# Attention with a routed expert gate on one Trainium2 core: values of two neighbouring pairs computed together from batch 1 on in place of batch 3

## The chip, the cores and the metric
The kernel is one program on one NeuronCore of a Trainium2 chip. The metric is device time in microseconds for one execution, lower is better. Engines: TensorE (PE, its weight loads PEld), VectorE (DVE), ScalarE (ACT), GpSimd (POOL), SyncE (SP, which issues most DMAs).

## What is computed
Eight batches of 256 tokens with 128 channels; 16 heads of size 64, latent key and value width 64; 8 experts.
```python
xn = layernorm(x)
q = rope(xn @ wq.T);  lat = xn @ w_kv_down.T
k = rope(lat @ w_k_up.T);  v = lat @ w_v_up.T
s = softmax(causal(q @ k.T / 8)) @ v @ wo.T          # per head, then joined
e = max(top2(xn @ gate_w + gate_b).indices)          # one expert per token
g = silu(2 * (gelu(xn @ w1[e] + b1[e]) @ w2[e] + b2[e]))
out = x + s * g
```

## The kernel before
**Slots.** The attention is cut into 64 slots g = 8 b + p: batch b of 8, pair of heads p of 8. Every engine has its own hand-written order of the slots (`slot(g)`), and semaphores tie the engines together. After slot 39 the experts run (22 tiles of 128 tokens), then slots 40 to 63, with the gate of each batch.

**One pair through the engines.** `project(m)` (TensorE) makes queries (m even) or keys (m odd) for two pairs, some 6 items ahead, so slot g projects m = g + 6. `rotate(m)` (VectorE, L585) multiplies the bank with the rotary table, and `rotated(m)` (GpSimd, L463) adds the halves; SyncE's `place` moves the result to `qk_sb`. `scores(g)` (TensorE, L1080 and L1082) is issued in slot g − 2. `row_max(g)` (VectorE, L594) adds the mask and takes row maxima, `exponentials(g, i)` (ScalarE, L885) follow for each head i of the pair, `denominators(g)` (VectorE, L601) is the reciprocal, `scale(g)` (GpSimd L474, in the slots with scatters and gathers partly VectorE L612 and ScalarE L898) makes the probabilities. `turn(g)` (TensorE, L1092) transposes them, `turned_probs(g)` (ScalarE, L907) copies them to `probsT`, which has four places. `values(g)` (TensorE, L1106 and L1108) multiplies them with the latents into `o_bank`, `ctx_out(g)` (ScalarE, L914) copies the result to `ctxT`, and `output(g)` (TensorE, L1120) multiplies by the joined value and output weights into `y_bank`. `take_y(b)` (VectorE, L761) copies a batch's eight summed outputs.

**Single and double values.** A pair in `ALONE` has its own call of `values`, with 256 and 128 columns a matmul, in slot g + 1, and its own copy in slot g + 2. Other pairs go by two, even and odd together: `values(g)` in slot g + 2 with 512 and 256 columns a matmul, one `ctx_out` of 512 columns in slot g + 3, then `output(g)` in slot g + 3 and `output(g + 1)` in slot g + 4. So with singles every slot has one call of `values`, and with doubles every even slot has one and the odd slots none. Before the change the pairs 0 to 23, 38, 39, 62 and 63 are alone.

**Order of work around it.** In `slot(g)` TensorE does scores(g + 2), project(g + 6), turn(g), some side work in early slots (input rows, latents, counts), output, values. VectorE does row_max(g + 2), denominators(g + 1), side work of the slot (statistics, normalisation, top 2, routing), and rotate(g + 6) last. In slots 8 to 20 all projections go into one bank, `j_bank`; from slot 20 on they alternate between two (`bank_of`). `project(m)` waits for `rope_done` at m while there is one bank (g up to TWO_J = 20), and at m − 1 from slot 21 on. In slots 22 to 37 GpSimd also issues a scatter of one tile of rows (L482).

Of the kernel before, what the change touches and what calls it, by code (L numbers as in the profile page):

```python
# [24 lines left out]
NP = H // 2  # L25
# [26 lines left out]
FINALS = {48: 0, 51: 5, 53: 1, 54: 2, 56: 3, 59: 6, 61: 4}  # L52
FINAL_ORDER = tuple(FINALS.values()) + (7,)
Z_PART = 18
FIRST_DOUBLE = 3 * NP
ALONE = tuple(range(FIRST_DOUBLE)) + (G_LEAD - 2, G_LEAD - 1, B * NP - 2, B * NP - 1)


# [37 lines left out]
def build(nc, x, wqT, w_dgT, w_kupT, w_vup, woT, gate_b, w1, b1, w2, b2,  # L96
          c_rot, c_ident, c_mask, c_before, c_expert, c_excl, c_incl, c_tile, out):
    with ExitStack() as ctx:
# [473 lines left out]
        def _(dve):  # L572
# [186 lines left out]
            def take_y(b):  # L759
                dve.wait_ge(y_step, NP * b + NP)  # L760
                dve.tensor_copy(y_keep[:, b, :], y_bank[:, 0:2 * C]).then_inc(y_read, 1)  # L761
# [16 lines left out]
            def slot(g):  # L778
                if 0 < g // NP < LEAD and g % NP == (2 if NP * (g // NP) <= FIRST_DOUBLE else 3):
                    take_y(g // NP - 1)  # L780
# [557 lines left out]
```

## Time and profile before

| | |
|---|---|
| Median of 3 runs (lowest, highest) | 310.27 us (310.02, 311.63) |
| Profiled execution: its time, its span | 311.37 us, 309.6 us |
| Busy, share of the span: PE, PEld | 96%, 77% |
| DVE, ACT, POOL | 71%, 78%, 70% |
| Mean granted TensorE clock | 0.985 of full speed |

The span goes from the first to the last instruction; the execution's own time holds what lies around it as well. Busy shares are averages over stages with different limits. Matmuls overlap in their pipeline, so the start of one group of matmuls to the start of the next says more about TensorE than the sum of durations.

### The profile page before, as it was taken

What the parts mean: (1) busy time and instruction counts of PE and PEld (TensorE: products, weight loads), DVE (VectorE), ACT (ScalarE), POOL (GpSimd) and SP (SyncE); (2) the same over time, 40 slices, a digit from 0 to 9 for tenths busy, and PEclk for the clock granted to TensorE, in tenths of its full rate; (3) what the DMA queues carried; (4) which work ended last, traced back from release to release, by engine and by line L of the source; (5) the groups of instructions that cost most, each with busy time, mean ns of one, the idle gap of its engine ahead of it and who ended that gap; (6) DMA issues with size and microseconds to landing.
All of it is one profiled execution on the core that took longest, in us unless ns stands there. A gap on an engine that the chain in (4) does not pass through costs nothing.

```text
span 309.6 us, 8479 instructions
## 1 busy us (share of the span) xinstructions
PE 296.1 (96%) x2358; PEld 237.5 (77%) x2358; DVE 221.1 (71%) x883; ACT 242.8 (78%) x851; POOL 215.8 (70%) x321
## 2 busy tenths in 40 slices
PE   8889999999999999999999989999989999899994
PEld 3578788888888888777777789999867777786763
DVE  4879998987787998988888523232268789898651
ACT  3376889898877789989897665555699999889982
POOL 3367978687777779999999943322138999889730
PEclk9987999999999999999999999999999999999998
DMA  6754595869433333333345470000063334344200
GB/s 207 231 135 112 96 263 151 216 168 298 113 69 71 65 73 86 95 87 87 88 101 138 124 210 0 2 2 0 3 186 71 89 103 112 105 109 131 74 18 18
DMA packets 39597, 33.35 MB, mean 108 GB/s; under 512 B 4802, under 2 KB 36675, under 8 KB 39555
## 3 DMA queue, kind: packets, MB, share of 16 engines
q1 hardware_dynamic: 38098, 30.51, 38.5%
q0 software_dynamic: 1024, 2.10, 2.5%
q8 instruction: 20, 0.33, 0.5%
q10 hardware_dynamic: 432, 0.23, 0.3%
q14 instruction: 23, 0.18, 0.2%
HBM read 11.07 MB, written 4.98 MB: 52 GB/s over the span
## 4 chain that ended last, share of the span: by engine, by line
PE 65%; POOL 12%; issue 11%; DVE 8%; ACT 2%; DMA 1%; POOLq 1%; SPq 0%; DVEq 0%; ACTq 0%
PE bank L1092 9%; PE bank L1080 9%; PE bank L1106 7%; PE bank L1120 6%; PE bank L1299 6%; PE bank L1284 6%; POOL probs L474 5%; POOL staged L463 4%; PE bank L1054 4%; PE bank L1082 3%; DVE rot_out L585 3%; PE bank L1108 3%; DVE masked L594 2%; PE bank L1070 2%; PE bank L1056 2%
## 5 line engine op out<-in xcount | busy, mean ns | idle before, releaser
L885 ACT ACTIVATE pexp<-masked,negmax 128x128 f32<-128x128 f32 (+1 forms) x256 | 114.1, 452 | 1.7 <-DVE negmax L594 1.6
L474 POOL TENSOR_SCALAR probs<-pexp,rden 128x256 f32<-128x256 f32 (+1 forms) x184 | 80.3, 451 | 27.0 <-DVE rden L601 24.2
L594 DVE CUSTOM_DVE_ANT_0 masked<-bank,mask 128x128 f32<-128x128 f32 (+1 forms) x256 | 75.9, 352 | 28.0 <-PE bank L1082 27.8
L463 POOL TENSOR_TENSOR staged<-rot_out 128x512 f32<-128x512 f32 x63 | 80.2, 1274 | 17.7 <-DVE rot_out L585 17.2
L585 DVE TENSOR_TENSOR rot_out<-bank,rot 128x1024 f32<-128x1024 f32 x64 | 77.7, 1215 | 4.0 <-PE bank L1056 2.7
L907 ACT COPY probsT<-bank 128x384 f32<-128x384 f32 x128 | 55.0, 480 | 23.8 <-PE bank L1092 23.2
L1092 PE MATMUL bank<-ident,probs 128*128 128x128 f32 x384 | 55.3, 278 | 1.8 <-ACT probsT L907 0.9
L885 ACT ACTIVATION_READ_ACCUMULATOR pexp<-masked,negmax 128x1 f32 x256 | 49.8, 195 | 0.0
L1080 PE MATMUL bank<-qk_sb 64*128 64x256 f32 x256 | 45.7, 434 | 2.6 <-DVE negmax L594 1.9
L1092 PEld LDWEIGHTS bank<-ident,probs 128*128 128x128 f32 x384 | 43.7, 141 | 5.0 <-POOL probs L474 1.8
L1120 PE MATMUL bank<-vo_sb,ctxT 128*128 128x128 f32 x256 | 39.5, 279 | 0.7 <-ACT ctxT L914 0.7
L1038 ACT ACTIVATE probsT<-bank,w_own 128x128 f32<-128x128 f32 x88 | 25.1, 368 | 18.8 <-PE bank L1284 18.8
L1106 PE MATMUL bank<-probsT,lat_all 128*64 128x256 f32 (+1 forms) x184 | 37.7, 488 | 0.3 <-ACT probsT L907 0.3
L1120 PEld LDWEIGHTS bank<-vo_sb,ctxT 128*128 128x128 f32 x256 | 33.7, 191 | 1.9 <-ACT ctxT L914 1.1
L549 POOL COPY w_own<-w_sb 128x516 f32 x22 | 13.5, 616 | 27.4 <-ACT probsT L1038 27.4
L1080 PEld LDWEIGHTS bank<-qk_sb 64*128 64x128 f32 x256 | 19.9, 188 | 16.2 <-issue 13.7
L1082 PEld LDWEIGHTS bank<-qk_sb 64*128 64x128 f32 x256 | 25.5, 190 | 2.7
L914 ACT COPY ctxT<-bank 128x256 f32<-128x256 f32 (+1 forms) x46 | 20.7, 451 | 6.8 <-PE bank L1108 5.6
L1082 PE MATMUL bank<-qk_sb 64*128 64x128 f32 x256 | 25.5, 275 | 0.0
L1299 PE MATMUL bank<-w_sb,probsT 128*128 x176 | 24.4, 282 | 0.7 <-issue 0.4
L1108 PEld LDWEIGHTS bank<-probsT,lat_all 128*64 128x64 f32 x184 | 13.3, 137 | 14.3 <-issue 10.3
L1284 PE MATMUL bank<-probsT,w_own 128*128 128x128 f32 x176 | 23.4, 277 | 0.7 <-DVE probsT L854 0.4
(113 smaller groups left out, 459.8 us busy)
## 6 DMA issues: line engine op xcount, KB each, us to landing
qk_sb<-staged SPq DMA_DIRECT2D x128, 128.0 KB, 2.6
w_sb<-in_w SPq DMA_DIRECT2D x2, 1024.0 KB, 5.8
w_sb<-in_w SPq DMA_DIRECT2D x4, 512.0 KB, 4.9
sorted_x<-z SPq DMA_DIRECT2D x1, 1408.0 KB, 7.9
sorted_g<-z SPq DMA_DIRECT2D x1, 1152.0 KB, 5.6
out<-res SPq DMA_DIRECT2D x8, 128.0 KB, 1.9
x_sb<-in_x SPq DMA_DIRECT2D x3, 256.0 KB, 3.2
rot<-in_c_rot SPq DMA_DIRECT2D x1, 512.0 KB, 5.6
```

What stands on the lines that cost most here:

```text
L463: pool.tensor_tensor(staged[:, n % 2, :, m % 2, :], rot_out[:, m % 2, :, 0:S], rot_out[:, m % 2, :, S:2 * S], op=ALU.add).then_inc(staged_ ...
L474: pool.tensor_scalar(probs[:, g % 2, i, c], pexp[:, g % 2, i, c], rden[:, g % 2, i, k:k + 1], 1.0, ALU.mult, ALU.mult).then_inc(probs_read ...
L585: dve.tensor_tensor(rot_out[:, m % 2], bank_of(m)[:].unsqueeze(1).broadcast_to([P, 2, 2 * S]), rot[:], op=ALU.mult).then_inc(rope_done, 1)
L594: t = dve.tensor_tensor_reduce(masked[:, g % 2, i, c], s_bank[i][:, c], mask[:, c], -1.0, -NEG * 1e8, ALU.add, ALU.min, negmax[:, g % 2, i ...
L885: e = act.activation(pexp[:, g % 2, i, c], masked[:, g % 2, i, c], ACT.Exp, bias=negmax[:, g % 2, i, k:k + 1], scale=-1.0, accum_out=rowsu ...
L907: act.copy(probsT[:, g % 4, i, :], t_bank[i][:, 0:SW]).then_inc(probsT_ready, 1)
L1080: pe.matmul(s_bank[i][:, P:SW], qk_sb[r, 0, p, P:S], qk_sb[r, 1, p, :], start=True, stop=True)
L1082: m = pe.matmul(s_bank[i][:, 0:P], qk_sb[r, 0, p, 0:P], qk_sb[r, 1, p, 0:P], start=True, stop=True)
L1092: t = pe.transpose(t_bank[i][:, k * P:(k + 1) * P], probs[:, g % 2, i, k * P:(k + 1) * P], ident[:])
L1106: pe.matmul(o[r, :, :], lat_all[:, 2 * b, :], probsT[:, pairs, i, 0:S], start=True, stop=False)
L1120: m = pe.matmul(y_bank[:, i * C:(i + 1) * C], ctxT[:, p, i * P:(i + 1) * P], vo_sb[:, p, :], start=(p == 0 and i == 0), stop=(p == NP - 1) ...
L1299: m = pe.matmul(bank[6 + i][:, 0:C], hidT[:, i, k, :], w2_sb[:, k, :, :].rearrange("p e c -> p (e c)")[:, bass.ds(e * C, C)], start=(k == ...
```

## The change
The pairs that are computed by two begin with batch 1 (pair 8) in place of batch 3 (pair 24).
```diff
-FIRST_DOUBLE = 3 * NP
+FIRST_DOUBLE = NP
 ALONE = tuple(range(FIRST_DOUBLE)) + (G_LEAD - 2, G_LEAD - 1, B * NP - 2, B * NP - 1)
```
NP is 8. `FIRST_DOUBLE` stands also in VectorE's order, where it sets in which slot of the next batch `take_y` comes:
```python
if 0 < g // NP < LEAD and g % NP == (2 if NP * (g // NP) <= FIRST_DOUBLE else 3):
    take_y(g // NP - 1)
```
With the new value, `take_y(1)` moves from slot 18 to 19 and `take_y(2)` from slot 26 to 27. All that tests for `ALONE` follows: `values`, `ctx_out`, `output` and the counts in `values_through`.

## Rows read from the trace of the kernel before

**Rows 1.** The page: busy time, share of the span, instructions of each engine.
```profile
PE 296.1 (96%) x2358; PEld 237.5 (77%) x2358; DVE 221.1 (71%) x883; ACT 242.8 (78%) x851; POOL 215.8 (70%) x321
```

**Rows 2.** Timeline, TensorE, slots 19 to 21: start us, duration us, what.
```profile
98.83 0.70 PE L1080 MATMUL bank<-qk_sb 64*128 64x256 f32 x4
...
104.58 0.61 PE L1120 MATMUL bank<-vo_sb,ctxT 128*128 128x128 f32 x4
...
105.12 0.65 PE L1106 MATMUL bank<-probsT,lat_all 128*64 128x256 f32 x4
...
105.92 0.70 PE L1080 MATMUL bank<-qk_sb 64*128 64x256 f32 x4
```

**Rows 3.** Timeline, TensorE, slots 29 to 31.
```profile
134.00 0.70 PE L1080 MATMUL bank<-qk_sb 64*128 64x256 f32 x4
...
139.50 1.08 PE L1106 MATMUL bank<-probsT,lat_all 128*64 128x512 f32 x4
...
140.94 0.70 PE L1080 MATMUL bank<-qk_sb 64*128 64x256 f32 x4
```

**Rows 4.** Context copies of ScalarE by source line: duration ns min/median/max.
```profile
L914 ACT COPY ctxT<-bank x46: 351/373/587, 30.7 to 305.2; 128x256 f32<-128x256 f32 x28, 128x512 f32<-128x512 f32 x18
```

**Rows 5.** Timeline, all engines, slots 9 and 10; idle time and releaser in brackets.
```profile
62.20 1.21 DVE L585 TENSOR_TENSOR rot_out<-bank,rot 128x1024 f32<-128x1024 f32 x1
...
63.46 0.19 PEld L1054 LDWEIGHTS bank<-xnT_h,wq_h 128*128 128x128 f32 x1 [0.29 <-DVE rot_out L585]
```

**Rows 6.** Timeline, all engines, from the odd slots 11 to 19.
```profile
69.34 1.20 DVE L585 TENSOR_TENSOR rot_out<-bank,rot 128x1024 f32<-128x1024 f32 x1
...
71.89 0.19 PEld L1054 LDWEIGHTS bank<-xnT_h,wq_h 128*128 128x128 f32 x1
...
78.22 1.22 DVE L585 TENSOR_TENSOR rot_out<-bank,rot 128x1024 f32<-128x1024 f32 x1
...
79.67 0.18 PEld L1054 LDWEIGHTS bank<-xnT_h,wq_h 128*128 128x128 f32 x1
...
85.94 1.22 DVE L585 TENSOR_TENSOR rot_out<-bank,rot 128x1024 f32<-128x1024 f32 x1
...
87.67 0.19 PEld L1054 LDWEIGHTS bank<-xnT_h,wq_h 128*128 128x128 f32 x1
...
91.46 0.29 DVE L594 CUSTOM_DVE_ANT_0 masked<-bank,mask 128x128 f32<-128x128 f32 x1 [0.59 <-PE bank L1082]
...
93.70 1.21 DVE L585 TENSOR_TENSOR rot_out<-bank,rot 128x1024 f32<-128x1024 f32 x1
...
94.83 0.41 DVE L761 COPY y_keep<-bank 128x256 f32<-128x256 f32 x1
...
94.96 0.18 PEld L1054 LDWEIGHTS bank<-xnT_h,wq_h 128*128 128x128 f32 x1 [0.33 <-DVE rot_out L585]
...
101.65 1.23 DVE L585 TENSOR_TENSOR rot_out<-bank,rot 128x1024 f32<-128x1024 f32 x1
...
103.10 0.19 PEld L1054 LDWEIGHTS bank<-xnT_h,wq_h 128*128 128x128 f32 x1
```

**Rows 7.** Timeline, VectorE and GpSimd, slots 21 and 22.
```profile
109.04 1.21 DVE L585 TENSOR_TENSOR rot_out<-bank,rot 128x1024 f32<-128x1024 f32 x1
...
110.32 0.29 DVE L594 CUSTOM_DVE_ANT_0 masked<-bank,mask 128x128 f32<-128x128 f32 x1
...
112.91 1.22 DVE L585 TENSOR_TENSOR rot_out<-bank,rot 128x1024 f32<-128x1024 f32 x1
...
114.21 1.28 POOL L463 TENSOR_TENSOR staged<-rot_out 128x512 f32<-128x512 f32 x1 [1.43 <-DVE rot_out L585]
```

**Rows 8.** Chain that ended last, in order of time: start us, us, what.
```profile
123.88 0.92 POOL probs L474 x2
...
126.69 2.87 DMA qk_sb<-staged
...
129.61 0.70 PE bank L1080 x4
```

## Prediction, made before the changed kernel ran
> **What bounds the kernel now.** I read the page first, then the waits, then the chain that ended last, then the timeline of slots 8 to 30 engine by engine. The page puts TensorE at 96% of the span, with VectorE, ScalarE and GpSimd at 70 to 78% [rows 1]. That says that TensorE sets the pace on the whole, not that it does so at every hand-over. The timeline gives the pace in the steady part: with single values, two slots take 105.92 − 98.83 = 7.09 us [rows 2]; with values of two pairs together, 140.94 − 134.00 = 6.94 us [rows 3]. The reader should see there how little separates the two forms, and that the double form makes the slots uneven.
>
> In slots 8 to 20 all projections share one bank. `project(m)` waits until `rotate` of every earlier item has read it (`rope_done` at m, for g up to TWO_J = 20). VectorE does that rotation last in its slot, after `row_max(g + 2)`, which itself starts only when the scores of that same slot are there: the rows show VectorE idle for 0.59 us until TensorE's L1082 is done [rows 6]. So there is a loop: scores of slot g, row maxima, side work of the slot, rotation, projection of slot g + 1. Twice it already sets the pace: the projection's weights wait 0.29 us for the rotation into slot 10 [rows 5] and 0.33 us into slot 18 [rows 6]. From slot 22 on two banks alternate, and the loop is gone.
>
> **What the change removes and saves.** Pairs 8 to 23 leave ALONE: 16 single calls become 8 double ones. On TensorE a single call takes 105.92 − 105.12 = 0.80 us from its first matmul to the next scores [rows 2], a double one 140.94 − 139.50 = 1.44 us [rows 3]. That is 2 × 0.80 − 1.44 = 0.16 us per pair of slots, 8 × 0.16 = 1.3 us in all, at most. The columns stay the same, and 8 recorded matmuls of 16 go (two calls of 4 L1106 and 4 L1108 become one), so about 20 ns for each that goes. On ScalarE, 16 copies of 256 columns become 8 of 512: 8 × (2 × 0.37 − 0.59) = 1.2 us less, from the median and the longest copy [rows 4]; ScalarE is not on the path, so this counts as nothing. If a late copy came before the exponentials, the cost would be at most 0.59 us in a slot, which I keep for a rival. `take_y` of batch 1 and 2 moves one slot later in VectorE's order, in front of the row maxima of slots 19 and 27. It is 0.41 us [rows 6]. In slot 18 it lies between rotation and row maxima, in slot 19 VectorE would be waiting for scores, so it costs nothing. No DMA is added or moved in its queue.
>
> **What it moves.** Work of values leaves the odd slots (9, 11, ..., 23) and doubles up in the even ones. An odd slot becomes 0.80 us shorter, the next even one 0.64 us longer. But the 0.80 us lay exactly between the scores of the odd slot and the projection of the even one, that is, beside the loop through VectorE. The loop does not shorten. What counts for each odd slot is the slack before: the projection's start minus the end of the rotation and 0.05 us of hand-over (63.46 − 62.20 − 1.21) [rows 5].
> - slot 9: no slack. New wait 0.80 us.
> - slot 11: 71.89 − 69.34 − 1.20 − 0.05 = 1.30 us [rows 6]. The slot also turns input rows; no wait.
> - slot 13: 79.67 − 78.22 − 1.22 − 0.05 = 0.18 us [rows 6]. New wait 0.62 us.
> - slot 15: 87.67 − 85.94 − 1.22 − 0.05 = 0.46 us. New wait 0.34 us.
> - slot 17: no slack (94.96 against 93.70 + 1.21 + 0.05). New wait 0.80 us.
> - slot 19: 103.10 − 101.65 − 1.23 − 0.05 = 0.17 us. New wait 0.63 us.
> - slots 21 and 23: two banks, so the projection waits for the rotation of one slot earlier; no wait.
>
> The sum is 0.80 + 0.62 + 0.34 + 0.80 + 0.63 = 3.19 us of new waiting. Against it, up to the scores of slot 21, TensorE has done 12 single calls fewer (slots 9 to 20, 12 × 0.80 = 9.60) and 6 double ones more (slots 10 to 20, 6 × 1.44 = 8.64), and is one `output` of 105.12 − 104.58 = 0.54 us behind [rows 2], since slot 10 has none. So it has 9.60 − 8.64 + 0.54 = 1.50 us less behind it. Slot 21 starts 3.19 − 1.50 = 1.69 us later, at 107.61 instead of 105.92. Both forms have served pairs 8 to 19 by then; only the one `output` is owed, and it comes in slot 26, which has none in the kernel before.
>
> **Where it goes after slot 21.** Slot 21 is a short one, and TensorE alone would come to slot 22 only 1.69 − 0.80 = 0.89 us late. But from here VectorE is the later one. Its rotation of slot 21 follows the scores by 109.04 − 105.92 = 3.12 us [rows 2, 7], so it comes at 110.73. Before, the next row maxima began at 110.32, 0.07 us after the rotation's recorded end at 110.25 [rows 7]; elsewhere VectorE's next work starts 0.08 us ahead of that end (94.83 against 93.70 + 1.21) [rows 6], so up to 0.15 us of waiting for scores vanishes. The rotation of slot 22 then comes at 110.73 + 3.87 − 0.15 = 114.45 against 112.91 [rows 7], 1.54 us later. GpSimd waits for just that rotation (1.43 us idle, then at work from 114.21) [rows 7], and slot 22 is its first with a scatter. From then on the chain that ended last runs through GpSimd without a gap, over the probabilities at 123.88 to the transfer of `qk_sb` at 126.69 and TensorE at 129.61 [rows 8]. So the delay at slot 22 is handed on whole, and reaches TensorE at slot 28. Behind it both forms are the same code and both were double already, with no slack on TensorE that could pay it back.
>
> The gain of 0.16 us for each of the pairs is inside this sum (six of them before slot 21; the last ones are hidden under GpSimd's chain). Result: **+1.5 us**. The profiled execution took 311.37 us with a span of 309.6 us; the median of the runs is 310.27 us, 1.1 us below it. The difference is carried over: span 311.1, median **311.8 us**. A measurement of this kernel can tell about 0.5%, 1.55 us, from no change, and my number lies just on that line.
>
> **The rivals.**
> - *VectorE's loop has room after all* (row maxima or the rotation start earlier than the rows let me think, or the wait on the bank is passed sooner). Then all double calls bring 0.16 us: 310.27 − 1.3 = 309.0 us. The 96% of TensorE and the smooth 6.94 us per two slots speak for it; against it speak the two waits already there in slots 10 and 18, and that the smooth stretch has two banks. It decides if the new waits together are under 1.5 us. Chance 0.07.
> - *The delay is partly paid back between slots 21 and 28.* TensorE's own work would let it off with the 0.89 us at slot 22, if GpSimd had some reserve in its scatters: 310.27 + 0.9 = 311.2 us. For it: VectorE's side work of slot 22 contains short waits on other engines. Against it: GpSimd's chain has no gap. Chance 0.20, for anything from 310.4 to 311.3.
> - *ScalarE joins the loop.* In odd slots the double copy (0.59 us) stands between the two heads' exponentials, and waits for the values at the end of the even slot. The reciprocals behind it stand before the rotation on VectorE. If this makes five waits longer by 0.2 to 0.4 us, the sum grows by 1 to 2 us: 312.8 to 313.8 us. For it: ScalarE is at 78% and has side work in slots 9, 13 and 15. Against it: slots 24 to 37 run so at full pace, with ScalarE scaling probabilities on top. Chance 0.13.
> - *A double call saves nothing worth naming*, because what goes is only the issue of 8 matmuls and not 0.16 us. With a double call of 1.58 us the six double calls before slot 21 cost 6 × 0.14 = 0.84 us more, which gives 311.8 + 0.8 = 312.6 us. Against it stand the 1.44 us read directly [rows 3]. Chance 0.03. The Trainium skill states such a gap: "TensorE: Matmul & The Clock Gate", section "Back-to-back issue gap", has N/2.4 + 2.5 ns for one matmul, so 8 fewer would save an estimated 0.02 us; the trace here shows 0.16 us and does not agree.
> - *As forecast*, 311.3 to 312.5 us: 0.57.
>
> **Range and chances.** The forecast is 311.8; 310.2 to 313.2 leaves out the gain and the upper half of the last rival's cases, and takes in the partial payback and the call that saves nothing. Faster by over 0.5% needs more than the whole possible gain: 0.03. Slower by over 0.5%, above 311.8: half of the forecast's own cases and all of the third rival's with a bit of spread, 0.48. The rest within 0.5%: 0.49.
>
> **What would show it.** In the changed profile TensorE's projection weights (L1054) should show idle time on `rot_out` L585 of 0.8 to 1.1 us into slots 10 and 18, 0.6 into 14 and 20, 0.3 into 16, some 3.5 us in all, and none into slot 12. Odd slots from 9 on should take 2.6 us plus their extras. Scores of slot 19 should come 1.2 us later than 98.83, those of slot 21 1.7 us later, GpSimd's first scatter 1.5 us later, and the offset should then stay the same to the end. If the idle time on `rot_out` is much under 3 us, the loop argument is wrong. If it is there and the end is not later, the hand-over to GpSimd is. If the reciprocals (L601) wait for `pexp`, ScalarE has joined the loop.

## The result and the profile after
The changed kernel takes 313.13 us (median of 20 runs) against 311.04 us for the kernel before (20 runs), ratio 1.0058 with a 95% interval of 1.0043 to 1.0073: **slower by 0.58%, 1.8 us**. (The two medians lie 2.1 us apart; the ratio with its interval is the better measure, and 1.8 us is worked out from it.) The forecast was +1.5 us, to 311.8 us. The profiled execution has a span of 311.5 us against 309.6 us.

The page after, busy time by engine. TensorE does 64 matmuls fewer and is busy 2.5 us less than in [rows 1], and yet the span is longer:
```profile
PE 293.6 (94%) x2294; PEld 232.9 (75%) x2294; DVE 220.8 (71%) x883; ACT 243.0 (78%) x843; POOL 215.8 (69%) x321
```
The wait of TensorE's projection weights for the rotation, after (us in total, times, longest). It was 1.7 us in 4 times before; here are 3 us more of it:
```profile
PEld bank L1054 <- DVE rot_out L585: 4.7, 7, 1.1
```
The timeline of the weight loads after, slots 10 to 20 and slot 24 (start us, duration us, what, and in brackets the idle time and who ended it). The L1054 lines answer to lines of [rows 5] and [rows 6]; the two L1080 lines are scores that wait for their keys and queries, at slots 14 and 24:
```profile
63.59 0.19 PEld L1054 LDWEIGHTS bank<-xnT_h,wq_h 128*128 128x128 f32 x1 [1.09 <-DVE rot_out L585]
...
78.46 0.30 PEld L1080 LDWEIGHTS bank<-qk_sb 64*128 64x128 f32 x4 [0.61 <-DMA qk_sb<-staged]
79.44 0.19 PEld L1054 LDWEIGHTS bank<-xnT_h,wq_h 128*128 128x128 f32 x1 [0.25 <-DVE rot_out L585]
...
87.63 0.19 PEld L1054 LDWEIGHTS bank<-xnT_h,wq_h 128*128 128x128 f32 x1 [0.47 <-DVE rot_out L585]
...
95.56 0.19 PEld L1054 LDWEIGHTS bank<-xnT_h,wq_h 128*128 128x128 f32 x1 [1.12 <-DVE rot_out L585]
...
104.16 0.19 PEld L1054 LDWEIGHTS bank<-xnT_h,wq_h 128*128 128x128 f32 x1 [0.75 <-DVE rot_out L585]
...
117.59 0.30 PEld L1080 LDWEIGHTS bank<-qk_sb 64*128 64x128 f32 x4 [0.54 <-DMA qk_sb<-staged]
```
TensorE waits at each even slot from 10 to 20 except 12, the one whose odd neighbour has little side work on VectorE (at slot 14 once for keys and once for the rotation). The chain that ended last shows what stands in the wait into slot 10: scores, row maxima, statistics, rotation, projection, with no slack between them:
```profile
59.84 0.24 PE bank L1082 x4
...
60.11 0.29 DVE masked L594
...
61.40 0.38 DVE st L620 x2
...
62.41 1.14 DVE rot_out L585
...
63.59 0.39 PE bank L1054
```
In [rows 8] the chain at that point of the kernel ran through GpSimd. After the change it goes, ahead of slot 24, through the sum, the queue and the transfer of the keys and queries rotated in slot 21:
```profile
112.03 1.28 POOL staged L463
...
113.33 0.59 SPq L363
...
113.97 3.59 DMA qk_sb<-staged
```

**One clock for all runs.** Executions differ by up to 1.7 us before slot 8, which has nothing to do with the edits. So from here on stages are counted from the start of slot 8, each worked out as one start in a trace (the first L1080 weight load of a slot, or VectorE's rotation of slot 22) minus the first L1080 weight load of slot 8. All from the one profiled execution of each kernel, in us. The ratios are against the kernel before as run again beside each:

| kernel | slot 21 | rotation of slot 22 | slot 28 | ratio to before, 95% interval |
|---|---|---|---|---|
| before | 51.26 | 58.25 | 74.95 | 1 |
| after | 52.83 | 59.68 | 76.66 | 1.0058 [1.0043, 1.0073] |
| e1 rotation first, 9 to 19 | 51.01 | 58.86 | 76.21 | 1.0051 [1.0029, 1.0073] |
| e2 the same, single values | 51.11 | 58.83 | 75.52 | 1.0005 [0.9982, 1.0028] |
| e3 values first | 50.06 | 57.35 | 74.63 | 0.9976 [0.9948, 1.0004] |
| e12 e3 again | 49.80 | 57.08 | 74.06 | 1.0000 [0.9979, 1.0020] |
| e4 doubles from pair 16 | 51.81 | 58.67 | 75.52 | 1.0034 [1.0006, 1.0062] |
| e5 doubles from pair 20 | 51.27 | 58.13 | 74.99 | 1.0017 [0.9997, 1.0037] |
| e6 e3 and rotation first, 21, 22 | 51.52 | 58.72 | 76.46 | 1.0015 [0.9992, 1.0039] |
| e7 rotation first 21, 22, single | 51.26 | 58.05 | 75.22 | 1.0003 [0.9984, 1.0022] |
| e8 rotation first, 15 and 19 | 52.11 | 59.96 | 76.79 | 1.0055 [1.0035, 1.0075] |
| e10 rotation first, 21 | 52.84 | 60.63 | 77.47 | 1.0113 [1.0085, 1.0140] |
| e9 e3 with the zero fill cut | 49.51 | 56.79 | 73.63 | 0.9964 [0.9938, 0.9990] |
| e11 zero fill cut, single | 51.26 | 58.24 | 74.93 | 1.0022 [1.0001, 1.0043] |

The interval of a ratio is 0.15 to 0.3% to each side, 0.5 to 0.9 us. A single transfer also came late in one profile and not in others: in e4, behind slot 28, slot 31 takes 3.49 us, of which TensorE waits 0.98 us for keys and queries; it takes 2.63 us in e5 and 2.67 us in the changed kernel.

### The profile page after: what moved, and what is told of

The parts are those of the page before. It is cut to its first block, busy times and chain, and to the rows that moved or that the text cites. A ratio compares the mean times of both kernels' runs of the same rounds, so it can differ in the third digit from the quotient of the medians.

```text
span 311.5 us, 8327 instructions
## 1 busy us (share of the span) xinstructions
PE 293.6 (94%) x2294; PEld 232.9 (75%) x2294; DVE 220.8 (71%) x883; ACT 243.0 (78%) x843; POOL 215.8 (69%) x321
## 4 chain that ended last, share of the span: by engine, by line
PE 66%; DVE 11%; issue 9%; POOL 8%; DMA 2%; ACT 1%; POOLq 1%; SPq 0%; DVEq 0%; ACTq 0%
PE bank L1092 10%; PE bank L1080 9%; PE bank L1106 8%; PE bank L1120 6%; PE bank L1299 6%; PE bank L1284 6%; DVE rot_out L585 4%; PE bank L1054 4%; PE bank L1108 3%; DVE masked L594 3%; PE bank L1082 3%; POOL probs L474 3%; POOL staged L463 3%; PE bank L1070 2%; PE bank L1056 2%
## 5 line engine op out<-in xcount | busy, mean ns | idle before, releaser
L474 POOL TENSOR_SCALAR probs<-pexp,rden 128x256 f32<-128x256 f32 (+1 forms) x184 | 80.3, 451 | 28.8 <-DVE rden L601 26.1
L1080 PE MATMUL bank<-qk_sb 64*128 64x256 f32 x256 | 46.0, 436 | 3.2 <-DVE negmax L594 2.1
L1106 PE MATMUL bank<-probsT,lat_all 128*64 128x512 f32 (+1 forms) x152 | 35.9, 550 | 0.3 <-ACT probsT L907 0.3
L1080 PEld LDWEIGHTS bank<-qk_sb 64*128 64x128 f32 x256 | 19.8, 188 | 18.2 <-issue 14.2
L914 ACT COPY ctxT<-bank 128x512 f32<-128x512 f32 (+1 forms) x38 | 19.6, 515 | 9.9 <-PE bank L1108 8.0
L1054 PE MATMUL bank<-xnT_h,wq_h 128*128 128x256 f32 x64 | 21.5, 337 | 3.9 <-DVE rot_out L585 3.8
```

Source lines behind the costliest of these rows:

```text
L474: pool.tensor_scalar(probs[:, g % 2, i, c], pexp[:, g % 2, i, c], rden[:, g % 2, i, k:k + 1], 1.0, ALU.mult, ALU.mult).then_inc(probs_read ...
L1080: pe.matmul(s_bank[i][:, P:SW], qk_sb[r, 0, p, P:S], qk_sb[r, 1, p, :], start=True, stop=True)
L1106: pe.matmul(o[r, :, :], lat_all[:, 2 * b, :], probsT[:, pairs, i, 0:S], start=True, stop=False)
```

## The experiments
**Theory.** One bank for projections up to slot 20 and VectorE's rotation last in its slot make a loop that the short odd slots run into. Rivals: ScalarE or GpSimd is late; VectorE is short of time altogether; the doubling itself costs. The most direct test, a second bank for the projections from slot 8 on, was not run.

**e3 and e12, values first.** TensorE gets the double values as work between scores and projection.
```diff
+VALUES_FIRST = (10, 12, 14, 16, 18, 20)
...
                 if g + 2 < B * NP:
                     scores(g + 2)
+                if g in VALUES_FIRST:
+                    values(g - 2)
...
-                if g > 1 and g % 2 == 0 and g - 2 not in ALONE and g != G_LEAD:
+                if g > 1 and g % 2 == 0 and g - 2 not in ALONE and g != G_LEAD and g not in VALUES_FIRST:
                     values(g - 2)
```


> The changed kernel, with the double values ahead of the projection in slots 10, 12, ..., 20, so that TensorE has 1.44 us of work between the scores and the projection while the rotation ends. Loop theory: the waits of 0.25 to 1.12 us are all shorter than 1.44 us and are covered; slot 21 starts near 104.1 and the time is 1 to 2 us below before. Rival (VectorE is simply short of time in these slots): the wait remains wherever the projection stands, and the time stays that of the changed kernel.

> e3 once more, for its size: the interval of e3 touched no change. Expected 0.3 to 0.9 us below before, from slot 28 coming 0.3 us earlier in its profile and its median 0.8 us lower.

Slot 21 comes 2.8 and 3.0 us earlier than in the changed kernel, and 1.2 and 1.5 us earlier than before. The timeline of e3's weight loads, slots 14 to 18:
```profile
77.32 0.30 PEld L1081 LDWEIGHTS bank<-qk_sb 64*128 64x128 f32 x4 [0.67 <-DMA qk_sb<-staged]
...
79.61 0.19 PEld L1055 LDWEIGHTS bank<-xnT_h,wq_h 128*128 128x128 f32 x1 [0.38 <-issue]
...
87.43 0.19 PEld L1055 LDWEIGHTS bank<-xnT_h,wq_h 128*128 128x128 f32 x1 [0.38 <-issue]
...
94.36 0.19 PEld L1055 LDWEIGHTS bank<-xnT_h,wq_h 128*128 128x128 f32 x1 [0.38 <-DVE rot_out L586]
```
(The line numbers are one higher, and 0.38 us is the ordinary idle time of a weight load behind double values, whether "issue" or another ended it.) The waits on the bank are gone, with the doubles and VectorE's order untouched. That shows the loop and its length; "VectorE is short of time" falls, since then the wait would have stayed. That one bank is what closes the loop is read from the code and from e5, not from a run with a second bank. The rest of the expectation, slot 21 near 104.1 (49.4 us after slot 8), was missed by the 0.67 us at slot 14, a wait for keys and queries. And of the gain at slot 21 only 0.3 to 0.9 us is left at slot 28: at slot 24 TensorE waits 1.27 us (e3) and 0.95 us (e12) for keys and queries. Both forecasts of the time missed: e3 is 0.24% below before (1 to 2 us had been expected), e12 is level with it; together no difference that can be told.

**e4 and e5, where doubling starts.** The one line `FIRST_DOUBLE = 2 * NP`, and `FIRST_DOUBLE = 20`.

> Doubles from pair 16 on (batch 2). Loop theory: only slots 17 and 19 are short slots with one bank, new waits 0.80 + 0.63 = 1.43 us; up to slot 21 four single calls fewer and two double ones more and one output behind, 3.20 - 2.88 + 0.54 = 0.86 us. Slot 21 comes 0.6 us later than 105.92, and the end is 0.3 to 0.9 us later than before. Rival (each doubled pair costs the same): half of the change's 16 pairs, so half of its loss, +0.9 us, with slot 21 near +0.85 us.

> Doubles from pair 20 on, so that the first short slot is 21, where projections already have two banks. Loop theory: no wait on rot_out beyond the two of the kernel before; slot 21 starts as before (51.3 us after slot 8). The rotation of slot 22, from which GpSimd's unbroken chain starts, comes as before, so slot 28 and the end come as before: within 0.3 us. Rival (doubling saves 0.16 us per pair wherever it is done): two double calls, 0.3 us faster. Rival (the first short slot costs, whatever the banks): +0.5 us or more.

e4: slot 21 +0.55 us, slot 28 +0.57 us, as the two short slots with one bank say (the rival had +0.85). Its time is +0.34%, 1.1 us, somewhat over the 0.3 to 0.9 us expected, with the late transfer at slot 31 in its profile; the time alone does not tell the theory from the rival, slot 21 does. e5: slot 21 +0.01 us, slot 28 +0.04 us, and a time within its interval of no change. So a doubled pair neither brings its 0.16 us here nor costs anything that can be told; the short slots below 21 cost.

**e1, e2 and e8, rotation first.** VectorE does `rotate` ahead of its side work.
```diff
+ROTATE_FIRST = (9, 13, 15, 17, 19)        # e8: (15, 19)
...
                     denominators(g + 1)
                     scale(g + 1)
+                early = g in ROTATE_FIRST
+                if early:
+                    for m in items(g):
+                        rotate(m)
...
-                for m in items(g):
-                    rotate(m)
+                if not early:
+                    for m in items(g):
+                        rotate(m)
```


> Loop theory (one bank, VectorE's rotation last): the changed kernel with the rotation ahead of VectorE's side work in slots 9, 13, 15, 17 and 19. The rotation then starts about 2.2 us after the scores of its slot, as in slot 11, and the projection finds the bank free: idle time of L1054 on rot_out in slots 10 to 20 under 0.3 us in all instead of 3.7. Slot 21 starts 3.19 + 0.38 us earlier than in the changed kernel, near 104.1, and the time is 1.5 to 2.1 us below the kernel before (ratio 0.993 to 0.995). Rival (ScalarE or GpSimd is late in the short slots): the idle time moves to other waits, and the time stays within 0.5 us of the changed kernel, +1.3 to +2.3 us against before.

> Control: the same order of VectorE in the kernel before (single values to pair 23). Loop theory: only the two waits of 0.29 and 0.33 us go, so -0.3 to -0.6 us against before. Rival (the order itself is what is worth something, doubles or not): the gain is like that of the doubled kernel with this order, -1.5 us or more.

> The changed kernel with the rotation ahead of the side work only in slots 15 and 19, whose side work (top values of batch rows, tile counts) nobody waits for at once. Loop theory: the waits of 0.47 us into slot 16 and 0.75 us into slot 20 go, those into 10, 14 and 18 stay; slot 21 comes 1.2 us earlier than in the changed kernel (51.6 us after slot 8 instead of 52.8), and the end is +0.3 to +0.9 us against before. Rival (another wait takes their place, as in e1): slot 21 comes less than 0.5 us earlier.

In e1 the waits into slots 10, 14, 16, 18 and 20 do vanish, and slot 21 comes 1.8 us earlier than after, not 3.6 us. New waits stand elsewhere: 0.62 us for a rotation into slot 11, 0.80 us for keys and queries at slot 14, and the token counts of slot 18 are late. At slot 22 the scores wait 0.55 us for row maxima. The time is that of the changed kernel: the theory's forecast of the time failed. e8 is the cleaner dose: from slot 16 to 17 it takes 4.30 instead of 4.65 us and from 20 to 21 4.30 instead of 4.94 us, so both waits are gone as expected, while slots 13 and 14 take 0.24 us more, for a later transfer at slot 14 in this execution. Slot 21 comes 0.7 us earlier than in the changed kernel, between the 1.2 us expected and the rival's limit of 0.5 us. But the rotation of slot 22 comes 0.28 us later, and the time is +0.55% (1.7 us) instead of the 0.3 to 0.9 us expected. The timeline of e8 in slot 19 shows why:
```profile
103.82 1.28 POOL L464 TENSOR_TENSOR staged<-rot_out 128x512 f32<-128x512 f32 x1
103.91 1.21 DVE L690 CAST tiles_f<-tiles_i 128x8 f32<-128x8 int32 x1
```
and the changed kernel in the same place, beside GpSimd's scaling (four instructions of L474 from 102.42 on, 1.66 us together):
```profile
102.62 0.23 DVE L689 CAST tiles_f<-tiles_i 128x8 f32<-128x8 int32 x1
```
A cast of 8 columns takes 1.21 us instead of 0.23 us: it started behind GpSimd's sum of a rotation and ends with it (103.82 + 1.28 = 105.10, 103.91 + 1.21 = 105.12). Work moved behind the rotation runs exactly when GpSimd adds up what was rotated. e1 and e2 have the same in slots 17 and 19 (casts of 1.18 to 1.22 us). So these three runs say less of the loop than of this collision. e2, the control, gives 0.15 us at slot 21, and is 0.6 us late at slot 28 for the same reason; its time is that of before, and the gain of 0.3 to 0.6 us that I expected isn't there.

**e6, e7 and e10, rotation first in slots 21 and 22.** The same edit with other slots: (21, 22) on top of e3, (21, 22) on the kernel before, (21,) on the changed kernel.

> The version with values first (e3), and VectorE's rotation ahead of the routing work in slots 21 and 22. In e3 TensorE waits 1.27 us for keys and queries at slot 24, whose rotation in slot 21 stands behind 0.95 us of routing work, and GpSimd waits 1.43 us for the rotation of slot 22. If this hand-over is what holds the end: the wait at slot 24 falls to about 0.3 us, slot 28 comes 0.9 to 1.2 us earlier than in e3 counted from slot 8, and the time is 1.3 to 2 us below before. Rival (the wait belongs to the transfer, 3.9 us long and slowed by its neighbours): the wait stays over 1 us and the time is that of e3, -0.7 us.

> Control: the kernel before with the rotation ahead of the routing work in slots 21 and 22 alone. GpSimd's chain starts about 1 us earlier, TensorE has 0.6 us of waiting in slots 25 to 28 to give back: -0.4 to -0.6 us. Rival (GpSimd's chain is not what sets slot 28): no change.

> The changed kernel with the rotation ahead of the routing work in slot 21 alone. The wait of 0.54 us for keys and queries at slot 24 should go, since their rotation comes 0.95 us earlier; GpSimd's chain from slot 22 on stays. Slot 28 then comes 1.5 us late against before instead of 1.7 us, and the time is 0.2 us below that of the changed kernel, +1.3 to +1.8 us against before. Rival (the transfer's own length sets it): the wait stays.

All three missed. e10 shows the mechanism best. The wait for the transfer at slot 24 is gone as expected, but the scores there still wait, now 0.64 us for row maxima (slot 24 begins 3.30 us after slot 23; without a wait it is 2.62 us). The routing cast that moved behind the rotation of slot 21 meets GpSimd's sum, and all that VectorE does next comes later:
```profile
111.26 1.27 POOL L464 TENSOR_TENSOR staged<-rot_out 128x512 f32<-128x512 f32 x1
111.30 1.26 DVE L706 CAST pos<-place_f 128x16 uint32<-128x16 f32 x1
```
In the changed kernel this cast runs beside GpSimd's scaling (L474, four instructions from 109.98 on, 1.62 us together) and takes a third of the time:
```profile
110.41 0.42 DVE L705 CAST pos<-place_f 128x16 uint32<-128x16 f32 x1
```
The cast is 0.84 us longer, the rotation of slot 22 comes 0.95 us later, and slot 28 comes 0.81 us later. Unwanted as it was, this tests the second half of the prediction: whether the rotation of slot 22 sets where slot 28 stands, through GpSimd. The timeline of e10's weight loads has the hand-over at the turn of slot 24:
```profile
119.64 0.31 PEld L1098 LDWEIGHTS bank<-ident,probs 128*128 128x128 f32 x3 [0.39 <-POOL probs L475]
```
The turn of slot 24 waits so for GpSimd's probabilities in e1, e4, e5, e8, e9 and e10, each time until 4.56 to 4.59 us after the rotation of slot 22. From there TensorE goes at its own pace, and slot 28 lies 16.83 to 16.86 us behind that rotation in all of them but e1. With single values (before, e2, e11) it is 16.7 us. In the remaining ones something else ends last: keys and queries at slot 24 in the changed kernel and e12 (16.98 us) and e3 (17.28 us), at slot 26 in e7 (17.17 us, a wait of 0.64 us), at slot 28 in e1 (17.35 us), and row maxima at slot 24 in e6 (17.74 us). e7 has the long cast too (1.28 us), so its rotation of slot 22 came only 0.2 us earlier than before, and slot 28 came 0.27 us later; what an earlier start of GpSimd is worth in the kernel before stays open. e6 lost 1.5 us at slot 14 to a transfer that was late in that execution and 0.84 us to the cast; its scores at slot 24 wait 1.42 us, for row maxima and no longer for the transfer, so it does not tell what it was to tell. e10's time, +1.1% (3.5 us, where 1.3 to 1.8 us was expected), is more than its profile shows (slot 28 at +0.81 us against the changed kernel, its span 0.6 us over it), with only 6 runs; that remainder is open.

**e9 and e11, the zero fill cut.** SyncE fills `sorted_x` with zeros in three transfers at slots 9, 13 and 17, and loads the biases at slot 15; e9 has it on top of e3, e11 on the kernel before.
```diff
+CLEARS = {9: (0, 8), 13: (8, 15), 17: (15, 22)}
...
-                if g in (1, 3, 5, 7, 9):
+                if g in (1, 3, 5, 7):
                     expert_weights(g // 2)
+                if g == 15:
+                    expert_weights(4)          # without the zero fill
+                if g in CLEARS:
+                    clear(*CLEARS[g])
...
-                    pool.wait_ge(zero_out, 16)
+                    pool.wait_ge(zero_out, 48)
```


> Values first (e3), and the zero fill of sorted_x (1408 KB in one transfer at slot 9) cut into three transfers at slots 9, 13 and 17, with the load of the biases at slot 15. If the wait of 0.67 us for keys and queries at slot 14 comes from those transfers beside it, it falls under 0.2 us, slot 21 comes 0.5 to 0.7 us earlier than in e3 (49.4 us after slot 8 instead of 50.06), and the time is 0.8 to 1.6 us below before. Rival (the short slot alone makes the wait): it stays at 0.5 us or more, and the time is that of e3.

> Control: the kernel before with the cut zero fill alone. It has no wait for keys and queries at slot 14, so nothing changes: within 0.3 us.

The biases (`b_all`, 512 KB) stood in the queue just ahead of the fill, so both are moved away from slot 14's keys. The wait at slot 14 is gone in e9: slot 14 begins 2.62 us after slot 13 (22.47 − 19.85 us after slot 8), the length of a short slot without a wait; in e3 it was 3.18 us. Slot 21 comes at 49.51 us, 1.75 us ahead of before, and slot 28 1.3 us ahead. One profile would not show the cause, since e10, with the fill in one piece, has no wait there either. SyncE's queue shows it. These are the four issues of keys and queries ahead of slot 14 (duration in ns, shortest, median and longest; first and last start in us), first in the changed kernel, then in e9:
```profile
L363 SPq DMA_DIRECT2D qk_sb<-staged x4: 613/619/2765, 72.6 to 76.7; - x4
...
L365 SPq DMA_DIRECT2D qk_sb<-staged x4: 590/608/612, 72.0 to 74.0; - x4
```
The fill of the changed kernel was issued at 69.7 us and landed 8.1 us later, so it is under way there. In all twelve profiles with the fill in one piece the longest of these four issues takes 1.57 to 3.44 us; in the two with the fill cut it takes 0.61 us. So the fill and the biases hold up the transfers behind them, and whether TensorE waits for it depends on how late the keys were to begin with. Which of the two does it was not separated.

The time is 0.36% below before (1.1 us; interval 0.1 to 0.6%): **e9 is the only run of the table whose interval lies below no change**, and it is clearly faster than the changed kernel. It can't be told from e3, whose interval (0.9948 to 1.0004) overlaps its own (0.9938 to 0.9990). The control without doubles gains nothing from the cut fill: 1.0022, if anything slower, with slots 21 and 28 where they were; no change had been expected.

## Why the prediction was right, point by point
- *The loop through the one bank.* Right in mechanism and nearly in every size. Predicted new waits were 0.80, 0.62, 0.34, 0.80 and 0.63 us, none into slot 12. Measured at the projection, beyond the 0.29 and 0.33 us that were there: 1.09 − 0.29 = 0.80 and 1.12 − 0.33 = 0.79 us into slots 10 and 18. For slots 16 and 20, where before the change 0.85 us lies between scores and projection (103.10 − 102.25 us into slot 20): 87.63 − 86.43 − 0.85 = 0.35 and 104.16 − 102.68 − 0.85 = 0.63 us. For slot 14 the wait is split: the scores came 3.12 instead of 2.63 us after those of slot 13, and the projection waited 0.13 us more, 0.62 us in all. The transfer that was late there cost nothing, because the rotation was just as late. e3 shows the cause by filling the wait, e4 and e5 by moving its start.
- *Slot 21 later by 1.69 us.* Measured 1.57 us.
- *The hand-over to GpSimd.* Predicted +1.54 us at the rotation of slot 22, measured +1.43 us. The way from there was not quite as written. The prediction has GpSimd hold TensorE all the way to slot 28, as in [rows 8]; in the doubled kernels TensorE meets GpSimd at the turn of slot 24 and is itself the longest chain from there. By that route, 16.85 us as in e4, e5, e8, e9 and e10, slot 28 of the changed kernel would stand at 59.68 + 16.85 = 76.53 us, 1.58 us late: an estimate from those runs. What I had not seen is a second path: the keys and queries rotated in slot 21 reach the scores only in slot 24, and with a double call in one slot of three TensorE gets there in 4.31 + 2 × 2.62 = 9.55 us instead of 10.5 us. The sum, queue and transfer (1.28 + 0.59 + 3.59 us) didn't fit, and TensorE waited 0.54 us. In the changed kernel this path ends last, just ahead of GpSimd's, and slot 28 came 1.71 us late. So this stretch of the sum was too small by about 0.2 us; it is luck that the two paths lie so close together that the forecast of the time hardly suffers. The remaining 0.1 us of the +1.8 us can't be told from noise.
- *Where the saving of 0.16 us per pair went.* It is in the sum, as forecast: TensorE is busy 2.5 us less on the page, and waits more. Where the waits are covered the saving shows: slots 19 and 20 take 2.63 + 4.31 = 6.94 us in e3 against 7.09 us before [rows 2].
- *The rivals.* That the loop has room: refuted, 3.2 us of new waits. That GpSimd pays some back: refuted, slot 22 comes 0.77 us later than before and slot 28 1.71 us. That ScalarE joins: in the changed kernel none of VectorE's reciprocals between 55 and 115 us waits for the exponentials. That a double call saves nothing: refuted by the same two slots of e3.
- *The time.* +1.5 us forecast, +1.8 us measured, interval 1.3 to 2.3 us. The absolute time was less well met: 313.13 us against 311.8 us, only just inside the stated 310.2 to 313.2 us. Over half of that comes from the base: the kernel before was taken at 310.27 us from 3 runs, and its median over 20 runs is 311.04 us. The chances were even between slower by over 0.5% (0.48) and no such change (0.49), and 0.58% favours the first only by a little; the slots are the real test.

## What to carry to other kernels
Before two short pieces of work are joined into one, look at what else runs while each is done: work moved out of a short stage cannot be saved there if the stage is held by a loop through another engine, and it comes back in full in the next stage. The slack of that loop, slot by slot, gives the cost before anything is built. If the joined piece is wanted all the same, put it where the wait is (here ahead of the projection), and then look for the next thing that the shorter way leaves no time for, here a transfer of 128 KB behind one of 1408 KB. Moving other work to make room is not free either: all six runs that reordered VectorE's work (e1, e2, e6, e7, e8, e10) met a cast that took 0.8 to 1 us longer, and none of the three that reordered only TensorE's did.

## What the runs showed of the hardware that was not expected
Some of VectorE's instructions wait for GpSimd's sum. A cast of 128x8 from int32 took 0.23 us beside GpSimd's scaling and 1.21 us when it started 0.09 us after the sum of 128x512 (L464); the cast of 128x16 to uint32 took 0.42 us and 1.26 us. Both end within 0.03 us of the sum's end. VectorE's scaling (L613 in e10), 0.29 us elsewhere, took 1.21 us from 0.14 us after the start of such a sum. VectorE's rotation, which reads PSUM, keeps its length: in the changed kernel one of 1.21 us began at 169.47, 0.39 us after a sum of 1.26 us. The Trainium skill, "SBUF — State Buffer", section "Who interferes with whom", says that a VectorE instruction in a two-port mode and GpSimd block each other for a whole instruction, whichever starts first; the runs agree for these casts, always with the sum first. Beside GpSimd's scaling (L474), whose single instructions are about 0.4 us long, the same casts took no more than their 0.23 and 0.42 us.
